# Attention scores on half the array's rows, and operand stacks copied inside SBUF

## The chip, the cores and the metric

One core of a Trainium2 chip runs the whole kernel. The metric is the device time of one launch in microseconds. TensorE, VectorE (DVE), ScalarE (ACT), GpSimd (POOL) and the DMA queue of SyncE (SP) each take their instructions in program order and wait for each other through semaphores.

## What is computed

The input x has 2048 tokens of 128 numbers. First comes causal attention with 16 heads of 8 dimensions, then a residual and a layer norm, then a mixture of 8 experts (each token goes to its best one) with a shared expert, a residual and a second layer norm. The change is in the attention:

```python
q, k, v = proj(Wq, bq), proj(Wk, bk), proj(Wv, bv)     # 16 heads of 8
scores = einsum('bhqd,bhkd->bhqk', q, k) / sqrt(8)     # masked: k_pos > q_pos
m = max(scores, axis=-1)
p = softmax(scores - m)
out = einsum('bhqk,bhkd->bhqd', p, v) @ Wo.T + bo
```

## The kernel before

Tokens go in 4 blocks (B) of 512, heads in 4 groups (g) of 4; a step is one group of one block (s = 4 B + g). q and k are float32, but the matmuls of scores take bf16: each number is split into three bf16 parts (ScalarE writes the first from the projection's PSUM bank, line 830; VectorE the other two, lines 942 to 947), and all nine products of parts are summed by stacking: q_stack and k_stack hold, per head, 9 x 8 = 72 rows (STACK), each row a part of one dimension. Three more rows hold the three bf16 parts of the row maxima, against rows of -1 in k_stack, so that one matmul gives scores minus maximum. 96 rows are contracted (KROWS); the rows from 64 on are filled beforehand (line 677, 680 on POOL, 932 on VectorE).

The stacks are built by DMA from SP's queue: send() writes the three parts of a side to memory (parts_dram, line 565), stack_q() reads them back in three DMAs of 24 rows (line 580), stack_k() in nine of 8 rows (line 591). Block 0 goes in two groups, heads 0 to 3 first. send(0, 1) and send(1, 1) follow; block 1's stack_q and stack_k are put on the queue after the maxima of step 0.

Each step runs through these items:

- scores (line 1230): for 128 queries t, a block c of up to 512 keys and a pair of heads hp, two matmuls q_stack x k_stack into two PSUM banks; on the diagonal (c == B) each is followed by a mask matmul of 128 columns (line 1233). VectorE takes the maxima of both banks (line 966). 320 such jobs, 288 of them in blocks 1 to 3.
- maxima: VectorE combines them (line 974), POOL splits them in three parts (lines 721, 726).
- maxrows: TensorE turns the parts (line 1241), ScalarE copies them to max_rows (line 850), SP sends them into q_stack (line 619).
- probs (line 1254): keys on the partitions, one matmul per head; ScalarE takes the exponential (line 843). It is scores minus maximum, recomputed in the other orientation. POOL masks the diagonal ones (line 710).
- values (line 1271): four heads at once, in four tiles of 32 columns of the array, f32.

make_plan writes one order for all of it: it goes through the probs items, each with a due count of score jobs (from columns, not from times), and lets a model of the engines' clocks choose between the next score job and the next main item. Every engine follows this order. SP follows it too, so a DMA waits on the queue for what stands before it:

```python
sp.wait_ge(max_rows_kept, s + 1)
sp.dma_start(q_stack[STACK:STACK + PARTS, B % 2, 4 * g:4 * g + 4, :], max_rows[:, s % 2, :])
if s == 0:
    stack_q(1, slice(0, H), q_stacked[1])
    stack_k(1, slice(0, H), k_stacked[1])
```

Of the kernel before, what the change touches and what calls it, by code (L numbers as in the profile page):

```python
# [28 lines left out]
JOB_COLUMNS = 60  # L29
LAST_RATE = 1.3  # L30
# [20 lines left out]
def make_plan(NB, G):  # L51
# [55 lines left out]
    plan, job, turns = [], 0, 0  # L107
# [17 lines left out]
    def put(item):  # L125
# [4 lines left out]
        if kind == "scores":  # L130
            _, m, B, g, t, c, hp = item
            w = width(B, t, c)
            clock["tensor"] += 0.84 * w + 8 + 107 * (c == B)
# [7 lines left out]
        elif kind == "probs":  # L141
            w = BLK - P * max(0, item[4] - TPB * item[2])
            clock["tensor"] += 0.42 * w + 3
# [4 lines left out]
        elif kind == "values":  # L148
            clock["tensor"] += 1.83 * (BLK - P * max(0, item[4] - TPB * item[2]))
        elif kind in costs:  # L150
            tensor, reader, read, after = costs[kind]
            clock["tensor"] += tensor
# [41 lines left out]
def block_kernel(nc, x, Wq, bq, Wk, bk, Wv, bv, Wo, bo, router_w, w_gate, w_up, w_down,  # L194
# [22 lines left out]
    SCALE = float(HD) ** -0.5  # L217
    STACK = PARTS * PARTS * HD
    KROWS = 96
    VC = HD + 1  # L220
    assert D == P and H * HD == D and STACK + PARTS <= KROWS
# [105 lines left out]
    with ctx:  # L327
# [24 lines left out]
        max_parts = sb("max_parts", [P, 2, TPB, PARTS, 4], BF16)  # L352
# [64 lines left out]
        parts_dram = nc.dram_tensor("parts_dram", (2, NB, PARTS, P, BLK), BF16, kind="Internal").ap()  # L417


# [22 lines left out]
        first_q_stacked = sem("first_q_stacked")  # L442
        first_k_stacked = sem("first_k_stacked")
# [17 lines left out]
        q_sent = [sem(f"q_sent{b}") for b in range(NB)]  # L461
        k_sent = [sem(f"k_sent{b}") for b in range(NB)]
# [77 lines left out]
        STACKED = 16  # L540
        CLEARED = 16
# [9 lines left out]
        def _(sp):  # L551
            sp.dma_start(x_sb[:, 0:TPB, :], x_tiles[:, 0:TPB, :]).then_inc(x_loaded[0], 16)
            sp.dma_start(w_nat[:, 1, :], Wk).then_inc(qk_loaded, 16)
            sp.dma_start(bias_qk[:, 1:2], bk.rearrange("(h d) -> d h", d=HD),
                         allow_slow_non_contiguous=True).then_inc(bias_qk_loaded, 16)
# [6 lines left out]
            def send(side, b):  # L562

                sp.wait_ge((q_split, k_split)[side], b + 1)
                sp.dma_start(parts_dram[side, b].rearrange("a p t -> p a t"),
                             qk_parts[:, side, b % 2, :, :]).then_inc((q_sent, k_sent)[side][b], 16)

            def stack_q(b, heads, stacked):

                sp.wait_ge(q_filled, min(b, 1) + 1)  # L570
                if b >= 2:

                    sp.wait_ge(exp_in_ready, units_before[b - 1])

                    sp.dma_start(q_stack[STACK:STACK + PARTS, b % 2, :, :],
                                 q_stack[STACK + PARTS:STACK + 2 * PARTS, b % 2, :, :]).then_inc(stacked, 16)
                sp.wait_ge(q_sent[b], 16)
                rows = parts_dram[0, b].rearrange("a (o d h) t -> o (a d) h t", o=1, d=HD)[:, :, heads, :]
                for r in range(PARTS):
                    sp.dma_start(q_stack[r * PARTS * HD:(r + 1) * PARTS * HD, b % 2, heads, :].rearrange("p h t -> p (h t)"),  # L580
                                 rows.rearrange("o p h t -> (o p) (h t)")).then_inc(stacked, 16)

            def stack_k(b, heads, stacked):

                sp.wait_ge(k_filled, b + 1)
                sp.wait_ge(k_sent[b], 16)
                for r in range(PARTS):
                    rows = parts_dram[1, b, r].rearrange("(d h) t -> d h t", d=HD)[:, heads, :].rearrange("d h t -> d (h t)")
                    for a in range(PARTS):
                        at = (r * PARTS + a) * HD  # L590
                        sp.dma_start(k_stack[at:at + HD, b, heads, :].rearrange("p h t -> p (h t)"), rows).then_inc(stacked, 16)
# [816 lines left out]
```

## Time and profile before

| | us |
|---|---|
| median of 3 runs | 608.11 (606.51 to 609.79) |
| profiled execution, its own time | 612.24 |
| its span, first to last instruction | 610.50 |
| TensorE / VectorE / ScalarE / POOL busy | 550.3 / 456.6 / 356.8 / 150.7 |

The rows further down come from the profiled execution. A busy time is the time in which an engine had at least one instruction under way; matmuls overlap, so the start times of neighbouring rows tell more of TensorE's pace than their lengths. PEclk is the granted clock of TensorE as a share of 2.4 GHz; the other level is 1.2 GHz, 0.50. "PEld" is the loading of weights, "SPq" the issue of a DMA on SP's queue. L1230 is line 1230 of the kernel before.

### The profile page before, as it was taken

What the parts mean: (1) busy time and instruction counts of PE and PEld (TensorE: products, weight loads), DVE (VectorE), ACT (ScalarE), POOL (GpSimd) and SP (SyncE); (2) the same over time, 40 slices, a digit from 0 to 9 for tenths busy, and PEclk for the clock granted to TensorE, in tenths of its full rate; (3) what the DMA queues carried; (4) which work ended last, traced back from release to release, by engine and by line L of the source; (5) the groups of instructions that cost most, each with busy time, mean ns of one, the idle gap of its engine ahead of it and who ended that gap; (6) DMA issues with size and microseconds to landing.
All of it is one profiled execution on the core that took longest, in us unless ns stands there. A gap on an engine that the chain in (4) does not pass through costs nothing.

```text
span 610.5 us, 10445 instructions
## 1 busy us (share of the span) xinstructions
PE 550.3 (90%) x3497; PEld 233.8 (38%) x3497; DVE 456.6 (75%) x765; ACT 356.8 (58%) x803; POOL 150.7 (25%) x267
## 2 busy tenths in 40 slices
PE   5539599999999999999999999999999899998980
PEld 3224234434333334333333333333434225664460
DVE  5728378999989988888888878888872515777684
ACT  3003355746567766877777776767778884331350
POOL 5651123130211202111001101101003157215644
PEclk9655789999999999999999999999999999999995
DMA  5736300036200045100000000000000111211233
GB/s 125 170 59 112 47 1 2 28 96 115 55 1 28 1 119 115 31 2 18 12 1 28 1 1 28 2 1 2 1 1 20 35 32 48 51 37 52 43 68 90
DMA packets 22909, 25.62 MB, mean 42 GB/s; under 512 B 2987, under 2 KB 21363, under 8 KB 22275
## 3 DMA queue, kind: packets, MB, share of 16 engines
q1 hardware_dynamic: 20896, 21.67, 15.2%
q0 software_dynamic: 1536, 3.15, 2.9%
q8 instruction: 29, 0.48, 0.3%
q14 instruction: 24, 0.19, 0.1%
q10 hardware_dynamic: 424, 0.13, 0.1%
HBM read 17.44 MB, written 7.21 MB: 40 GB/s over the span
## 4 chain that ended last, share of the span: by engine, by line
PE 73%; DVE 10%; DMA 6%; issue 5%; POOL 3%; ACT 2%; SPq 0%; POOLq 0%; DVEq 0%; ACTq 0%
PE out_ps L1271 21%; PE score_ps L1230 19%; PE ring_ps L1254 19%; DVE part_max L966 5%; DMA q_stack<-max_rows 3%; PE score_ps L1360 3%; PE score_ps L1233 2%; PE ring_ps L1377 1%; PE ring_ps L1280 1%; POOL k_stack L789 1%; PE score_ps L1312 1%; POOL qk_parts L776 1%; PE score_ps L1254 1%; PE ring_ps L1195 1%; PE ring_ps L1241 1%
## 5 line engine op out<-in xcount | busy, mean ns | idle before, releaser
L966 DVE TENSOR_REDUCE part_max<-score_ps 128x2 f32<-128x1024 f32 (+3 forms) x320 | 327.7, 1062 | 75.3 <-PE score_ps L1233 45.8
L843 ACT ACTIVATE probs<-ring_ps 128x512 f32<-128x512 f32 (+3 forms) x611 | 285.1, 537 | 123.9 <-PE ring_ps L1254 121.8
L1230 PE MATMUL score_ps<-k_stack,q_stack 96*128 96x512 bf16 (+3 forms) x640 | 182.3, 364 | 19.0 <-issue 10.5
L1254 PE MATMUL ring_ps<-q_stack,k_stack 96*128 96x512 bf16 (+3 forms) x611 | 172.9, 353 | 7.4 <-DMA q_stack<-max_rows 5.7
L1271 PE MATMUL out_ps<-probs,v_aug 128*32 128x512 f32 (+3 forms) x1280 | 150.7, 543 | 4.3 <-POOL probs L710 3.8
L1230 PEld LDWEIGHTS score_ps<-k_stack,q_stack 96*128 96x128 bf16 x640 | 60.5, 101 | 107.9 <-DVE part_max L966 39.2
L1254 PEld LDWEIGHTS ring_ps<-q_stack,k_stack 96*128 96x128 bf16 x611 | 52.1, 98 | 120.3 <-ACT probs L843 69.4
L710 POOL TENSOR_SCALAR_AFFINE_SELECT probs<-probs 128x512 f32<-128x512 f32 x64 | 40.6, 634 | 165.2 <-ACT probs L843 165.0
L1233 PE MATMUL score_ps<-mask_qk,ident_bf 128*128 128x128 bf16 x256 | 57.1, 241 | 0.0
L1271 PEld LDWEIGHTS out_ps<-probs,v_aug 128*32 128x32 f32 x1280 | 25.4, 108 | 49.6 <-issue 23.8
L721 POOL CAST max_parts<-row_max 128x16 bf16<-128x16 f32 x48 | 9.4, 196 | 117.7 <-DVE row_max L974 115.6
L776 POOL DMA_INDIRECT qk_parts<-xs_dram,q_stack x30 | 30.6, 1021 | 25.6 <-DVE q_stack L1093 17.7
L731 POOL TENSOR_TENSOR rstd<-rstd,minus_half 128x1 f32<-128x1 f32 x16 | 8.9, 554 | 103.3 <-DVE rstd L926 103.3
L1360 PE MATMUL score_ps<-w_gu,qk_parts 128*128 x60 | 32.0, 615 | 0.0
L850 ACT ACTIVATE max_rows<-ring_ps 12x512 bf16<-12x512 f32 x15 | 8.8, 584 | 39.0 <-PE ring_ps L1241 38.8
L1233 PEld LDWEIGHTS score_ps<-mask_qk,ident_bf 128*128 128x128 bf16 x256 | 27.6, 108 | 6.9 <-issue 0.9
L896 ACT ACTIVATE qk_parts<-score_ps 128x256 f32<-128x256 f32 x30 | 11.5, 384 | 29.3 <-PE score_ps L1360 29.3
L1111 DVE SCALAR_TENSOR_TENSOR qk_parts<-qk_parts,score_ps 128x256 f32<-128x256 f32 x30 | 12.6, 419 | 15.1 <-ACT qk_parts L896 15.0
L789 POOL DMA_INDIRECT k_stack<-sorted_dram,q_stack x16 | 16.9, 1054 | 15.3 <-DMA sorted_dram<-q_stack 10.6
L1377 PE MATMUL ring_ps<-wd,q_stack 128*128 x116 | 18.7, 284 | 0.2
L1377 PEld LDWEIGHTS ring_ps<-wd,q_stack 128*128 128x128 f32 x116 | 15.2, 191 | 1.6 <-issue 0.9
L877 ACT ACTIVATE k_stack<-score_ps 128x512 f32<-128x512 f32 x8 | 4.8, 597 | 18.0 <-PE score_ps L1312 18.0
(179 smaller groups left out, 417.6 us busy)
## 6 DMA issues: line engine op xcount, KB each, us to landing
q_stack<-parts_dram SPq DMA_DIRECT2D x9, 384.0 KB
k_stack<-parts_dram SPq DMA_DIRECT2D x27, 128.0 KB
parts_dram<-qk_parts SPq DMA_DIRECT2D x8, 384.0 KB, 2.7
sorted_dram<-q_stack SPq DMA_DIRECT2D x30, 64.0 KB, 1.5
x_sb<-in_L_attn_x_dram SPq DMA_DIRECT2D x4, 256.0 KB, 5.2
w_gu<-n_L_ffn_expert_gate_dram SPq DMA_DIRECT2D x8, 128.0 KB, 2.2
w_gu<-in_L_ffn_expert_up_dram SPq DMA_DIRECT2D x8, 128.0 KB, 2.4
wd<-n_L_ffn_expert_down_dram SPq DMA_DIRECT2D x8, 128.0 KB, 2.3
```

The costliest lines, as they stand in the source:

```text
L710: pool.affine_select(out=square, in_=square, compare_op=ALU.is_ge, fill=0.0, base=0, pattern=[[0, 4], [1, P]], channel_multiplier=-1).then ...
L776: pool.indirect_dma_start(out=xg[:, k % 8, :], out_offset=None, in_=xs_dram[0:P * tiles[w][1], :], in_offset=bass.IndirectOffsetOnAxis(ap= ...
L789: pool.indirect_dma_start(out=yg[:, t, :], out_offset=None, in_=sorted_dram[w][:, :], in_offset=bass.IndirectOffsetOnAxis(ap=slot_i[:, t:t ...
L843: act.activation(probs[:, n % RING, 0:w], bank(it)[:, 0:w], ACT.Exp, scale=SCALE).then_inc(probs_ready, 1)
L966: dve.tensor_reduce(out=part_max[:, s % 2, t, 2 * hp:2 * hp + 2, c], in_=score_ps[:, m % 2, :, 0:w], axis=AX.X, op=ALU.max).then_inc(score ...
L1111: link(dve.scalar_tensor_tensor(out=x_hid[:, k % 4, :], in0=x_hid[:, k % 4, :], scalar=1.0, in1=both[:, 0:FF], op0=ALU.add, op1=ALU.mult))
L1230: last = mm(score_ps[:, m % 2, i, 0:w], q_stack[0:KROWS, B % 2, h, t * P:(t + 1) * P], k_stack[0:KROWS, c, h, 0:w], start=True, stop=c < B)
L1233: last = mm(score_ps[:, m % 2, i, w - P:w], ident_bf[:, :], mask_qk[:, :], start=False, stop=True)
L1254: mm(bank(it)[:, 0:w], k_stack[0:KROWS, j // TPB, h, j % TPB * P:(j % TPB + 1) * P], q_stack[0:KROWS, B % 2, h, skip:BLK], start=True, sto ...
L1271: last = mm(out_ps[32 * i:32 * i + 32, skip:BLK], v_aug[:, j, h * VC:h * VC + 32], probs[:, (4 * k + i) % RING, 0:w], start=j == 0, stop=j ...
L1360: mm(bank(it), xgT[:, k % 4, :], w_gu[:, bass.ds(e, 1), :].rearrange("p a n -> p (a n)"), start=True, stop=True).then_inc(gate_up_made, 1)
L1377: last = mm(bank(it)[:, 0:D], x_hidT[:, k % 2, f * P:(f + 1) * P], wd[:, bass.ds(e, 1), f, :].rearrange("p a n -> p (a n)"), start=f == 0, ...
```

## The change

Two things change together, since both come from how the stacks lie.

The stacks are copied inside SBUF. send() and parts_dram are gone; stack_block(b) issues, for each of the three parts, each side, each half of the heads (x) and each of the three places where the part occurs, one DMA of 64 partitions x 512 bf16 into 8 rows x 8 heads x 512: 36 DMAs of 64 KB a block. It starts with the part that ScalarE writes, as soon as that stands, and ends with the smallest. Block 0 is no longer split into two groups of heads.

The heads lie in two halves. Heads 0 to 7 keep rows 0 to 95; heads 8 to 15 have their 72 rows at 56 to 127, with the maxima at 53 to 55 and the rest filled (zeros against -1). In each half the eight products of parts without the smallest one lie in 64 rows of one half of the array (0 to 63, 64 to 127). The score matmuls, which serve the maxima alone, contract only these 64 rows, and a job pairs a head of the lower half with one of the upper half. The mask matmuls come after both. Probs still contract all rows (96 or 128). max_rows goes into q_stack in two DMAs instead of one. The planner's clock charges 107 ns (DRAIN) where the tile shape changes, and 0.42 instead of 0.84 ns per score column.

```diff
-            clock["tensor"] += 0.84 * w + 8 + 107 * (c == B)
+            clock["tensor"] += drain(64, P if c == B else 64) + 0.42 * w + (DRAIN + 107) * (c == B)
...
-            clock["tensor"] += 1.83 * (BLK - P * max(0, item[4] - TPB * item[2]))
+            clock["tensor"] += drain(32, 32) + 1.67 * (BLK - P * max(0, item[4] - TPB * item[2]))
...
+    HALF = H // 2
+    LOW_TOP = 96
+    UP_AT = P - STACK
+    def head(g, i):
+        return 2 * g + i % 2 + HALF * (i // 2)
+    def rows_of(h):
+        return slice(0, LOW_TOP) if h < HALF else slice(0, P)
...
-            sp.dma_start(bias_qk[:, 1:2], bk.rearrange("(h d) -> d h", d=HD),
-                         allow_slow_non_contiguous=True).then_inc(bias_qk_loaded, 16)
+            for x in range(2):
+                sp.dma_start(bias_qk[64 * x:64 * (x + 1), 1:2], bk[64 * x:64 * (x + 1)].rearrange("(h d) -> d h", d=HD),
+                             allow_slow_non_contiguous=True).then_inc(bias_qk_loaded, 16)
...
+            def stack_block(b):
+                for part in reversed(range(PARTS)):
+                    for side in range(2):
+                        to, stacked = ((q_stack, q_stacked), (k_stack, k_stacked))[side]
+                        if part == PARTS - 1:
+                            sp.wait_ge(first_part_kept, 2 * b + side + 1)
+                        else:
+                            sp.wait_ge((q_split, k_split)[side], (PARTS - 1) * b + PARTS - 1 - part)
+                        if side == 0 and b >= 2:
+                            sp.wait_ge(exp_in_ready, units_before[b - 1])
+                        if part == 0:
+                            sp.wait_ge((q_filled, k_filled)[side], 2 * (min(b, 1), b)[side] + 2)
+                        for x in range(2):
+                            for other in reversed(range(PARTS)):
+                                r, a = ((other, part), (part, other))[side]
+                                at = (r * PARTS + a) * HD
+                                at = (at - HD) % STACK if x == 0 else UP_AT + at
+                                sp.dma_start(to[at:at + HD, (b % 2, b)[side], HALF * x:HALF * (x + 1), :],
+                                             qk_parts[64 * x:64 * (x + 1), side, b % 2, part, :]).then_inc(stacked[b], 16)
...
-            send(0, 0)
-            send(1, 0)
-            stack_q(0, slice(0, 4), first_q_stacked)
-            stack_k(0, slice(0, 4), first_k_stacked)
-            stack_q(0, slice(4, H), q_stacked[0])
-            stack_k(0, slice(4, H), k_stacked[0])
-            send(0, 1)
-            send(1, 1)
+            stack_block(0)
...
-                    sp.dma_start(q_stack[STACK:STACK + PARTS, B % 2, 4 * g:4 * g + 4, :],
-                                 max_rows[:, s % 2, :]).then_inc(max_rows_placed[s % 2], 16)
+                    sp.dma_start(q_stack[STACK:STACK + PARTS, B % 2, 2 * g:2 * g + 2, :],
+                                 max_rows[0:2 * PARTS, s % 2, :]).then_inc(max_rows_placed[s % 2], 16)
+                    sp.dma_start(q_stack[UP_AT - PARTS:UP_AT, B % 2, HALF + 2 * g:HALF + 2 * g + 2, :],
+                                 max_rows[2 * PARTS:4 * PARTS, s % 2, :]).then_inc(max_rows_placed[s % 2], 16)
                     if s == 0:
-                        stack_q(1, slice(0, H), q_stacked[1])
-                        stack_k(1, slice(0, H), k_stacked[1])
+                        stack_block(1)
...
-                    pool.memset(q_stack[64:96, 1, :, :].bitcast(F32), 0.0).then_inc(q_filled, 1)
+                    pool.memset(q_stack[64:96, 1, 0:HALF, :].bitcast(F32), 0.0).then_inc(q_filled, 1)
+                    pool.memset(q_stack[0:64, 1, HALF:H, :].bitcast(F32), 0.0).then_inc(q_filled, 1)
...
-                act.activation(wT[:, i, :].rearrange("p (d h) -> p d h", d=HD),
-                               score_ps[:, 1, 0, i * D:(i + 1) * D].rearrange("p (h d) -> p d h", d=HD), ACT.Copy).then_inc(w_kept, 1)
+                for x in range(2):
+                    half = slice(i * D + 64 * x, i * D + 64 * (x + 1))
+                    last = act.activation(wT[:, i, 64 * x:64 * (x + 1)].rearrange("p (d h) -> p d h", d=HD),
+                                          score_ps[:, 1, 0, half].rearrange("p (h d) -> p d h", d=HD), ACT.Copy)
+                last.then_inc(w_kept, 1)
...
-                    if B == 0 and g == 0 and t == 0:
-                        pe.wait_ge(first_k_stacked, STACKED * PARTS * PARTS)
-                        pe.wait_ge(first_q_stacked, STACKED * PARTS)
-                    elif g == (1 if B == 0 else 0) and t == 0:
-                        pe.wait_ge(k_stacked[c], STACKED * PARTS * PARTS)
-                        pe.wait_ge(q_stacked[B], STACKED * PARTS + (CLEARED if B >= 2 else 0))
-                    for i in range(2):
-                        h = 4 * g + 2 * hp + i
-                        last = mm(score_ps[:, m % 2, i, 0:w], q_stack[0:KROWS, B % 2, h, t * P:(t + 1) * P],
-                                  k_stack[0:KROWS, c, h, 0:w], start=True, stop=c < B)
-                        if c == B:
+                    if g == 0 and t == 0:
+                        pe.wait_ge(k_stacked[c], STACKED)
+                        pe.wait_ge(q_stacked[B], STACKED)
+                    for i, half in enumerate((slice(0, 64), slice(64, P))):
+                        h = head(g, 2 * i + hp)
+                        last = mm(score_ps[:, m % 2, i, 0:w], q_stack[half, B % 2, h, t * P:(t + 1) * P],
+                                  k_stack[half, c, h, 0:w], start=True, stop=c < B)
+                    if c == B:
+                        for i in range(2):
                             last = mm(score_ps[:, m % 2, i, w - P:w], ident_bf[:, :], mask_qk[:, :],
                                       start=False, stop=True)
```

## Rows read from the trace of the kernel before

**Rows 1.** Page, engines over the span: busy us, share, instructions

```profile
PE 550.3 (90%) x3497; PEld 233.8 (38%) x3497; DVE 456.6 (75%) x765; ACT 356.8 (58%) x803; POOL 150.7 (25%) x267
```

**Rows 2.** Busy time by stage: stretch, its length, engines; clock, DMA share, GB/s

```profile
20.00:80.00 60.00, 38.90 (x216) 18.70 (x217) 32.70 (x47) 11.77 (x27) 24.09 (x42) 0.59 0.46 85
130.00:182.00 52.00, 49.66 (x347) 21.06 (x345) 47.87 (x73) 31.32 (x72) 9.77 (x22) 1.00 0.35 71
283.00:455.00 172.00, 171.90 (x1115) 61.16 (x1114) 144.43 (x160) 127.14 (x264) 16.48 (x40) 1.00 0.03 8
73.40:80.00 6.60, 6.57 (x32) 2.81 (x33) 2.85 (x4) 3.87 (x8) 0.63 (x1) 0.50 0.01 2
```

**Rows 3.** Chain of waits, 20 to 80 us: start us, us, what

```profile
19.71 2.06 DMA k_stack<-parts_dram
...
30.32 9.14 issue
...
52.68 20.62 DMA q_stack<-max_rows
```

**Rows 4.** Timeline of TensorE in the steady stage: start us, us, what

```profile
308.60 0.64 PE L1271 MATMUL out_ps<-probs,v_aug 128*32 128x256 f32 x8
309.17 0.39 PE L1254 MATMUL ring_ps<-q_stack,k_stack 96*128 96x512 bf16 x1
...
312.90 0.38 PE L1254 MATMUL ring_ps<-q_stack,k_stack 96*128 96x512 bf16 x1
313.21 1.06 PE L1271 MATMUL out_ps<-probs,v_aug 128*32 128x512 f32 x8
314.21 0.61 PE L1230 MATMUL score_ps<-k_stack,q_stack 96*128 96x512 bf16 x2
314.65 0.38 PE L1254 MATMUL ring_ps<-q_stack,k_stack 96*128 96x512 bf16 x1
```

**Rows 5.** Groups by shape, line 1230: count, busy us, mean ns, idle before

```profile
L1230 PE MATMUL score_ps<-k_stack,q_stack 96*128 96x512 bf16 x448 | 135.9, 389 | 0.5 <-DVE part_max L966 0.2
...
L1230 PE MATMUL score_ps<-k_stack,q_stack 96*128 96x128 bf16 x64 | 12.2, 247 | 17.8 <-issue 10.5 <-DMA k_stack<-parts_dram 5.2 <-DVE part_max L966 2.0
```

**Rows 6.** SP's DMA queue, 10 to 135 us: start us, issue us, what

```profile
17.04 2.97 SPq L591 DMA_DIRECT2D k_stack<-parts_dram  x9
...
44.38 0.83 SPq L619 DMA_DIRECT2D q_stack<-max_rows  x1
...
46.59 3.07 SPq L591 DMA_DIRECT2D k_stack<-parts_dram  x9
...
131.75 0.71 SPq L575 DMA_DIRECT2D q_stack<-q_stack  x1
```

**Rows 7.** Stretches by what their DMA does; columns as in rows 2

```profile
17.25:20.75 3.50, 0.00 (x0) 0.00 (x0) 3.36 (x9) 0.00 (x0) 0.27 (x1) 0.96 0.34 95
46.00:48.00 2.00, 1.60 (x8) 0.59 (x6) 1.99 (x2) 0.00 (x0) 0.00 (x0) 0.50 0.81 189
60.00:68.00 8.00, 6.26 (x50) 2.37 (x48) 6.39 (x7) 3.55 (x11) 2.83 (x8) 1.00 0.51 71
415.55:415.75 0.20, 0.20 (x3) 0.08 (x2) 0.00 (x0) 0.20 (x1) 0.00 (x0) 1.00 0.18 61
```

**Rows 8.** Timelines of the first 80 us, four engines

```profile
8.71 0.69 ACT L830 ACTIVATE qk_parts<-ring_ps,bias_qk 128x512 bf16<-128x512 f32 x1 [2.23 <-PE ring_ps L1195]
...
13.71 0.43 DVE L947 CAST qk_parts<-qk_f 128x512 bf16<-128x512 f32 x1
...
30.34 0.18 DVE L974 TENSOR_REDUCE row_max<-part_max 128x16 f32<-128x16 f32 x1
...
38.81 0.20 POOL L721 CAST max_parts<-row_max 128x16 bf16<-128x16 f32 x1
...
67.11 0.64 PE L1271 MATMUL out_ps<-probs,v_aug 128*32 128x256 f32 x8 [1.23 <-POOL probs L710]
73.43 1.01 PE L1254 MATMUL ring_ps<-q_stack,k_stack 96*128 96x512 bf16 x2 [5.68 <-DMA q_stack<-max_rows]
```

More of the change, by code:

```diff
@@ L106, in make_plan, with drain @@
     slots, ring, exp_done, max_ready, max_placed = [0.0, 0.0], [0.0] * 3, {}, {}, {}
-    plan, job, turns = [], 0, 0
+    plan, job, turns, tiles = [], 0, 0, P
+    def drain(before, after):
+        nonlocal tiles
+        last, tiles = tiles, after
+        return DRAIN if before != last else 0
     def start_of(item):
@@ L142, in put @@
             w = BLK - P * max(0, item[4] - TPB * item[2])
-            clock["tensor"] += 0.42 * w + 3
+            clock["tensor"] += drain(P, P) + 0.42 * w + 3
             clock["scalar"] = max(clock["scalar"], clock["tensor"] + LATENCY) + 0.83 * w + 52
@@ L560, in _ @@
                              x_tiles[:, TPB * b:TPB * b + TPB, :]).then_inc(x_loaded[b], 16)
[L562 to L591, printed above, removed]
+            def stack_block(b):
[17 more added lines that the diff above has]
+                                             qk_parts[64 * x:64 * (x + 1), side, b % 2, part, :]).then_inc(stacked[b], 16)
@@ L717, in _ @@
                         pool.wait_ge(max_turned, s - 1)
-                    rest = row_max[:, s % 2, :, :]
+                    rest = row_max[:, s % 2, :, :].rearrange("p t (x j) -> p t x j", x=2)
                     for a in range(PARTS):
-                        part = max_parts[:, s % 2, :, a, :]
+                        part = max_parts[:, s % 2, :, :, a, :]
                         copied = pool.tensor_copy(part, rest)
@@ L826, in _ @@
                     if b == 0:
-                        act.wait_ge(bias_qk_loaded, 32)
+                        act.wait_ge(bias_qk_loaded, 64)
                     if b >= 2:
-                        act.wait_ge((q_sent, k_sent)[side][b - 2], 16)
-                    act.activation(qk_parts[:, side, b % 2, 0, :], bank(it), ACT.Identity,
+                        act.wait_ge((q_stacked, k_stacked)[side][b - 2], STACKED)
+                    act.activation(qk_parts[:, side, b % 2, PARTS - 1, :], bank(it), ACT.Identity,
                                    bias=bias_qk[:, side:side + 1]).then_inc(first_part_kept, 1)
@@ L941, in _ @@
                     parts = qk_parts[:, side, b % 2, :, :]
-                    dve.scalar_tensor_tensor(out=rest, in0=bank(it), scalar=bias_qk[:, side:side + 1], in1=parts[:, 0, :],
+                    dve.scalar_tensor_tensor(out=rest, in0=bank(it), scalar=bias_qk[:, side:side + 1], in1=parts[:, 2, :],
                                              op0=ALU.add, op1=ALU.subtract).then_inc(qk_kept, 1)
                     dve.wait_ge(qk_kept, 2 * b + side + 1)
-                    link(dve.tensor_copy(parts[:, 1, :], rest))
+                    split = (q_split, k_split)[side]
+                    dve.tensor_copy(parts[:, 1, :], rest).then_inc(split, 1)
+                    dve.wait_ge(split, (PARTS - 1) * b + 1)
                     link(dve.tensor_tensor(rest, rest, parts[:, 1, :], ALU.subtract))
-                    dve.tensor_copy(parts[:, 2, :], rest).then_inc((q_split, k_split)[side], 1)
+                    dve.tensor_copy(parts[:, 0, :], rest).then_inc(split, 1)
                 elif kind == "v_in":
@@ L1249, in _ @@
                     w = BLK - skip
-                    h = 4 * g + i
+                    h = head(g, i)
                     wait_bank(it)
                     if j == 0 and i == 0:
-                        pe.wait_ge(max_rows_placed[s % 2], 16 * (s // 2 + 1))
-                    mm(bank(it)[:, 0:w], k_stack[0:KROWS, j // TPB, h, j % TPB * P:(j % TPB + 1) * P],
-                       q_stack[0:KROWS, B % 2, h, skip:BLK], start=True, stop=True).then_inc(exp_in_ready, 1)
+                        pe.wait_ge(max_rows_placed[s % 2], 32 * (s // 2 + 1))
+                    mm(bank(it)[:, 0:w], k_stack[rows_of(h), j // TPB, h, j % TPB * P:(j % TPB + 1) * P],
+                       q_stack[rows_of(h), B % 2, h, skip:BLK], start=True, stop=True).then_inc(exp_in_ready, 1)
                 elif kind == "values":
```

54 lines of the change are left out of this document (24 added, 30 removed).

## The prediction, made before the change was run

> **What bounds the kernel now.** I read the page's engine table first [rows 1]: TensorE is busy for 90% of the span, VectorE for 75%, ScalarE for 58%. That is an average over stages, so next came the busy time by stage [rows 2]. From 283 to 455 us TensorE is busy for 171.90 of 172 us at the full clock, with VectorE at 84% and ScalarE at 74%: there only TensorE's own work counts, and a microsecond taken from it is a microsecond of the span as long as less than 16% goes. From 130 to 182 us it is busy for 96% and VectorE for 92%. From 20 to 80 us the picture is another one: TensorE 65%, a granted clock of 0.59, DMA busy. The chain of waits says why [rows 3]. The first scores wait for the DMA of the k stack until 21.8; then 9.14 us are waited for the other heads' stack (shown as "issue"); and from 52.68 to 73.30 one small DMA, the maxima of step 1 on their way into q_stack, takes 20.62 us, because block 1's stack was put on the same queue before it. So the change has two places to act in, and they are priced apart: the start (DMA) and the scores of blocks 1 to 3 (TensorE).
>
> **The scores.** TensorE streams the 512-column score matmuls 0.215 us apart (314.21 to 314.65 for two) [rows 4]. There are 448 such matmuls and 64 each of 384, 256 and 128 columns (the first and the last of four groups in [rows 5]), 278,528 columns; 20,480 are block 0's (32 jobs, two heads, four widths), so blocks 1 to 3 have 258,048, or 504 times 512. Two heads at once takes away half of that: 252 x 0.215 = 54.2 us, if the two halves truly run side by side. The trace has a pattern for that: the values put four heads in four column tiles of the array, and four 128x512 f32 matmuls of 0.6 us each, in two passes, end within 1.06 us [rows 4].
>
> The same rows price the other side. A 512-column probs matmul is followed by the next one after 0.215 us, but by values after 0.31 (312.90 to 313.21): 0.095 us to enter the other tile shape. The next matmul starts 1.00 us after values of 512 columns and 0.57 us after values of 256 (308.60 to 309.17); the line through the two has 1.68 ns a column and 0.14 us at zero columns, which is the price of leaving. So a switch costs 0.095 to 0.14 us; I take 0.11, nearer to the entry, since the exit also holds the staggered start of four tiles. The page TensorEngine Tiling (Array Packing) of the Trainium skill says under Key Properties that a change of the tiling mode, and not merely of the tile, drains TensorE; the trace agrees with these 0.095 us. Without that rule the scores part would be the whole 54 us.
>
> How many switches are new? The order that make_plan writes for the kernel before has 254 separate runs of score jobs in blocks 1 to 3 for 288 jobs: nearly every job stands alone between probs. Only 62 of the run ends touch values, where the array switches anyway. In blocks 1 to 3 the order has 313 changes of tile shape now; with scores in half-height tiles, and the mask matmuls of the 96 diagonal jobs in the full shape, the same order has 784. That is 471 new ones: 51.8 us at 0.11 (44.7 at 0.095, 65.9 at 0.14). The planner's due times count columns, which the diff leaves alone, so I expect about the same order. Against 54.2 us saved this is a gain of 2 us, between a gain of 10 and a loss of 12. If the second half had to wait for its own weight load, up to 0.055 us a job would come on top (16 us for 288); mask matmuls of 128 columns follow each other at such a pace with a weight load each, and that load can hide under the first half, so I take nothing and keep it as a bound.
>
> **The stack copies.** Per block the send, three q and nine k DMAs (with the split of block 0 into two groups) become 36 copies of 64 KB, 2304 KB as before. Three prices set how long they take.
> Issue: nine k copies took 2.97 and 3.07 us on SP's queue, 0.33 each; but the two kinds of DMA inside SBUF that the trace has, max_rows and the clearing of q_stack, took 0.83 and 0.71 [rows 6]. These go from three rows, so the cause may be the odd count. Bounds: 12 and 27 us for 36.
> Transfer: the k copies go to 8 rows at a time and use 8 of 16 DMA engines, as the new ones will; while only they ran they moved 71 GB/s (60 to 68 us, share 0.51) [rows 7]: 33 us for a block. The small first group went at 95 GB/s with share 0.34, held by issue. The one SBUF-to-SBUF row, max_rows in 1 KB pieces as in the new copies, moved 61 GB/s at a share of 0.18, 21 GB/s an engine: 8 engines would need 14 us.
> So a block takes 14 to 33 us. I take 20, between the nearest in kind (max_rows) and the nearest in pattern (k).
>
> With 20 us, step by step: q's first part stands at 9.40 and the last part of k at 14.14 [rows 8]; the second wT and bias pieces add some 0.5 us, so the copies run from 9.9 to 30 and land at 32 (2 us as in [rows 3]). That is later than the 21.8 of before, but all heads are there, and the 9.14 us wait is gone: step 0's scores took 8.5 us (21.8 to 30.34), so step 1 starts near 40, as it does now (30.32 + 9.14). POOL's fills and maxima, done at 39.0 [rows 8], cover nothing any more; POOL does the same fills in two halves each, at the same cost. max_rows of step 0 goes out near 45, now as two DMAs (0.8 us more); then SP issues block 1's copies, 46.4 to 66.4, and the maxima of step 1, queued behind them on SP and in the rings, land at 68.4 instead of 73.3. TensorE, whose last work before the stall ends at 67.8 [rows 8], then hardly waits: 5 us gained, and 2 more because the clock need not fall: after 5.68 us of standing still [rows 8] it was granted 0.50, that is 1.2 of 2.4 GHz, from 73.4 to 80, with TensorE busy all the time [rows 2]. For blocks 2 and 3 the copies have some 25 us before the next maxima are used, and the scores there wait for VectorE; nothing. Later max_rows DMAs cost 0.8 us of SP each, under those leads; if the lead were gone it would be 14 x 0.8 = 11 us. VectorE's and GpSimd's instructions keep their sizes.
>
> **Sum.** 2 us from the scores and 7 from the start: 9 us. The profiled execution has its own time of 612.24 us (span 610.50, 1.74 around it); 612.24 - 9 = 603.2. It lies 4.1 us above the median of the three runs, 608.11, so the median becomes 599.
>
> **The rivals.**
> A, the copies keep pace with issue: 14 us a block. First scores at 26, step 1's maxima in place at 58 and no stall; TensorE reaches that point at 63, as POOL at 39.0 holds step 0's maxima. That is 10 us, 3 for the clock and 2 from the scores: 593, down to 585 with switches at 0.095. The max_rows row speaks for it, the k rows against it.
> B, the slower end: the copies crowd into 8 rows each, in at 71 GB/s, or SP needs 0.75 us for each; 31 us a block. First scores at 43, block 1's copies from 57 to 88, step 1's maxima at 90: 16 us later than now, so 608 + 16 - 2 = 622. It decides from about 24 us a block on, where the landing (28 us and two blocks' copies after the start) passes 76. For it speaks that q's copies, to 24 rows, moved 189 GB/s (share 0.81) where k's, to 8, moved 71 [rows 7]; against it the 95 GB/s of the first group. The page SBUF — State Buffer of the Trainium skill (Door 1: The DMA port swizzle) has bandwidth follow the number of SBUF ports that a range of partitions reaches; by its 27 GB/s a port the two ports of 8 rows would give an estimated 43 us a block. The k rows, at 71 GB/s, lie above that and below q's.
> C, the two halves do not overlap, so the scores' part of the change does not do what it says: 52 us of switches for nothing, less 7: 653. The values' overlap speaks against it.
> D, a switch costs 0.14 us or the second weight load shows: a loss of 12 to 16 in blocks 1 to 3, less 7 at the start: 615.
>
> **How the numbers follow.** Forecast 0.40 (592 to 605), A 0.22, B 0.20, D 0.13, C 0.05. The range of 585 to 622 leaves out C, the half of B with still slower copies (0.10), and 0.04 at the foot of A. A change under 0.5% (3 us) is about what a measurement here cannot tell from none. Faster: A, and nearly all of the forecast: 0.60; same: the forecast's upper edge and the near edges of B and D: 0.10; slower: the rest, 0.30.
>
> **What would show it.** First scores at 32 us (A 26, B 43), and a 36-copy block of 20 us on SP; the DMA wait for max_rows near nothing in the chain, and a clock that stays up through 80 us. In the steady stage two score matmuls of one job starting together, gaps of about 0.1 us before and after each job, and TensorE still busy throughout, so a stretch that shrinks by little. Wrong it would be with SBUF copies far from 20 us a block, or gaps away from 0.11 us: 0.01 us of a gap is 5 us of the kernel.

## The result and the profile of the changed kernel

| | kernel before | changed kernel |
|---|---|---|
| median of 4 runs, us | 607.62 | 635.08 |
| ratio, with its 95% interval | | 1.0455 (1.0408 to 1.0502) |
| profiled execution, us | 612.24 | 632.4 |
| its span, us | 610.50 | 630.7 |

The change makes the kernel slower by 27.5 us where 9 us of gain were forecast. The two profiled executions lie nearer together than the medians (before's 4.6 us above its median, this one 2.7 below): the two traces hold 20.2 us of the loss. The kernel before spreads from run to run, most on the chip of the experiments with rows 8 apart (598.4 to 613.0 us), and a ratio with its interval may leave out longer runs, so that it can differ from the quotient of the medians.

Busy time by stage of the changed kernel, the stretches that [rows 2] show of before (columns: stretch, length, busy us of TensorE, its weight loads, VectorE, ScalarE and GpSimd; granted clock, DMA share, GB/s):

```profile
20.00:80.00 60.00, 29.59 (x168) 9.96 (x168) 27.15 (x41) 7.21 (x15) 22.16 (x41) 0.54 0.41 51
130.00:182.00 52.00, 42.92 (x277) 14.44 (x276) 40.76 (x58) 25.17 (x54) 7.40 (x18) 0.90 0.49 68
283.00:455.00 172.00, 171.10 (x1146) 48.98 (x1148) 146.89 (x165) 127.54 (x269) 19.02 (x44) 1.00 0.03 8
```

The steady stage is as full as it was. The two stages in which copies run are not: TensorE has 9.3 us less work done by 80 us and 6.7 us less between 130 and 182, where it was busy for 49.66 of 52 us before. SP's queue says when the copies go (start, time to issue, what):

```profile
9.40 3.98 SPq L593 DMA_DIRECT2D q_stack<-qk_parts  x6
...
29.18 3.89 SPq L593 DMA_DIRECT2D k_stack<-qk_parts  x6
58.27 0.79 SPq L611 DMA_DIRECT2D q_stack<-max_rows  x1
59.10 0.73 SPq L613 DMA_DIRECT2D q_stack<-max_rows  x1
59.88 3.98 SPq L593 DMA_DIRECT2D q_stack<-qk_parts  x6
...
84.31 0.76 SPq L611 DMA_DIRECT2D q_stack<-max_rows  x1
...
139.42 4.00 SPq L593 DMA_DIRECT2D q_stack<-qk_parts  x6
...
159.47 3.90 SPq L593 DMA_DIRECT2D k_stack<-qk_parts  x6
163.41 0.77 SPq L611 DMA_DIRECT2D q_stack<-max_rows  x1
...
178.03 0.72 SPq L611 DMA_DIRECT2D q_stack<-max_rows  x1
...
435.54 0.72 SPq L611 DMA_DIRECT2D q_stack<-max_rows  x1
```

The 36 copies of a block take 23.7 us to issue, 0.65 us each, and they land later than that by the chain of waits (start, us, what):

```profile
32.46 13.73 DMA k_stack<-qk_parts
...
85.11 5.60 DMA q_stack<-max_rows
...
158.75 13.03 DMA q_stack<-qk_parts
```

Block 0's last copy lands at 46.2, 13.7 us after it was issued and 36.8 us after the first: 2304 KB (2.36 MB) at 64 GB/s. A backlog has built up behind the issue. The first scores start at 46.3, the maxima of step 1 land at 90.7 (before: 73.3 [rows 3]), and block 2's copies land at 171.8 with TensorE waiting. In TensorE's timeline (start, us, what, then in brackets its idle time before and what ended that):

```profile
46.29 0.29 PE L1229 MATMUL score_ps<-k_stack,q_stack 64*128 64x128 bf16 x2 [29.76 <-DMA k_stack<-qk_parts]
...
171.91 0.61 PE L1229 MATMUL score_ps<-k_stack,q_stack 64*128 64x512 bf16 x2 [6.91 <-DMA q_stack<-qk_parts]
```

The maxima's DMAs, one step after the other, are milestones for where the loss arises. SP's queue of the kernel before (steps 5, 7 and 14), then step 5 of the changed kernel, whose others stand above:

```profile
114.34 0.70 SPq L619 DMA_DIRECT2D q_stack<-max_rows  x1
...
155.16 0.72 SPq L619 DMA_DIRECT2D q_stack<-max_rows  x1
...
414.20 0.72 SPq L619 DMA_DIRECT2D q_stack<-max_rows  x1
```

```profile
128.55 0.69 SPq L611 DMA_DIRECT2D q_stack<-max_rows  x1
```

Step 0's went out at 44.38 before [rows 6] and at 58.27 now: 13.9 us later. Step 5's is 14.2 us later, step 7's 22.9, step 14's 21.3, the end 20.2. So 14 us are lost at the start, some 9 more between steps 5 and 7, where block 2's stack is late, and then 2.7 us come back.

### The profile page after: what moved, and what is told of

Read it like the earlier page. It is cut to its first block, busy times and chain, and to the rows that moved or that the text cites. A ratio compares the mean times of both kernels' runs of the same rounds, so it can differ in the third digit from the quotient of the medians.

```text
span 630.7 us, 10545 instructions
## 1 busy us (share of the span) xinstructions
PE 545.3 (86%) x3497; PEld 198.0 (31%) x3497; DVE 455.7 (72%) x766; ACT 357.7 (57%) x805; POOL 151.0 (24%) x272
## 4 chain that ended last, share of the span: by engine, by line
PE 64%; SPq 10%; DVE 9%; DMA 7%; issue 4%; POOL 3%; ACT 2%; POOLq 0%; DVEq 0%; ACTq 0%
PE out_ps L1271 19%; PE ring_ps L1254 18%; PE score_ps L1229 11%; SPq L593 9%; DVE part_max L967 5%; PE score_ps L1233 3%; PE score_ps L1361 2%; DMA k_stack<-qk_parts 2%; DMA q_stack<-qk_parts 2%; PE ring_ps L1378 1%; PE ring_ps L1281 1%; POOL k_stack L783 1%; DMA q_stack<-max_rows 1%; PE score_ps L1313 1%; PE ring_ps L1196 1%
## 5 line engine op out<-in xcount | busy, mean ns | idle before, releaser
L1254 PE MATMUL ring_ps<-q_stack,k_stack 128*128 128x512 bf16 (+7 forms) x611 | 177.0, 358 | 2.1 <-ACT probs L841 1.3
L1229 PE MATMUL score_ps<-k_stack,q_stack 64*128 64x512 bf16 (+3 forms) x640 | 115.5, 371 | 50.3 <-DMA k_stack<-qk_parts 29.8
L1254 PEld LDWEIGHTS ring_ps<-q_stack,k_stack 96*128 96x128 bf16 (+1 forms) x611 | 48.6, 98 | 126.6 <-ACT probs L841 78.4
L1229 PEld LDWEIGHTS score_ps<-k_stack,q_stack 64*128 64x128 bf16 x640 | 29.7, 94 | 152.5 <-issue 86.7
L1233 PE MATMUL score_ps<-mask_qk,ident_bf 128*128 128x128 bf16 x256 | 40.0, 243 | 0.0
L770 POOL DMA_INDIRECT qk_parts<-xs_dram,q_stack x30 | 30.6, 1019 | 25.6 <-DVE q_stack L1094 17.7
L1233 PEld LDWEIGHTS score_ps<-mask_qk,ident_bf 128*128 128x128 bf16 x256 | 15.1, 100 | 23.6 <-issue 18.5
L841 ACT ACTIVATE probs<-score_ps 128x512 f32<-128x512 f32 (+3 forms) x29 | 15.2, 553 | 0.1
```

Source lines behind the costliest of these rows:

```text
L770: pool.indirect_dma_start(out=xg[:, k % 8, :], out_offset=None, in_=xs_dram[0:P * tiles[w][1], :], in_offset=bass.IndirectOffsetOnAxis(ap= ...
L841: act.activation(probs[:, n % RING, 0:w], bank(it)[:, 0:w], ACT.Exp, scale=SCALE).then_inc(probs_ready, 1)
L1229: last = mm(score_ps[:, m % 2, i, 0:w], q_stack[half, B % 2, h, t * P:(t + 1) * P], k_stack[half, c, h, 0:w], start=True, stop=c < B)
L1233: last = mm(score_ps[:, m % 2, i, w - P:w], ident_bf[:, :], mask_qk[:, :], start=False, stop=True)
L1254: mm(bank(it)[:, 0:w], k_stack[rows_of(h), j // TPB, h, j % TPB * P:(j % TPB + 1) * P], q_stack[rows_of(h), B % 2, h, skip:BLK], start=Tru ...
```

## The experiments

**The two halves of the change, one at a time.** The first kernel keeps the scores from 64 rows and builds the stacks through memory (`stack` reads a side's parts back into the new rows, for the given heads of each half):

```
+            def send(side, b):
+                sp.wait_ge((q_split, k_split)[side], (PARTS - 1) * (b + 1))
+                for x in range(2):
+                    sp.dma_start(parts_dram[side, b, x].rearrange("a p t -> p a t"),
+                                 qk_parts[64 * x:64 * (x + 1), side, b % 2, :, :]).then_inc((q_sent, k_sent)[side][b], 16)
...
-            stack_block(0)
+            send(0, 0)
+            send(1, 0)
+            stack(0, 0, 0, 2, first_q_stacked)
+            stack(1, 0, 0, 2, first_k_stacked)
+            stack(0, 0, 2, HALF, q_stacked[0])
+            stack(1, 0, 2, HALF, k_stacked[0])
...
```

> The scores from 64 rows, two heads at once, are kept; the stack rows go through memory again as in the kernel before (three q and nine k reads for each half of the heads, 25 reads a block where before had 12, with 8 KB a row in place of 16). Theory 1, the copies are the whole loss and the scores are worth next to nothing: 598 to 612 us, first scores near 32 us, TensorE again at 48 to 50 busy us of 52 in the second block's stage, and the steady stage 2 us shorter than before's. Rival, the half-height scores cost as well (a switch dearer than the 0.105 us that the timeline of the changed kernel shows): 615 to 630 us, and the distance from step 6 to step 15 longer than before's.

Measured: 606.99 us against 609.2 of before beside it, ratio 0.9967 (0.9931 to 1.0002). The scores, with the reads that their layout asks for, cost nothing; a gain of 2 us is not clear of none. So nothing in the loss is theirs. The second kernel keeps the copies and scores full rows:

```
-                    for i, half in enumerate((slice(0, 64), slice(64, P))):
+                    for i in range(2):
                         h = head(g, 2 * i + hp)
-                        last = mm(score_ps[:, m % 2, i, 0:w], q_stack[half, B % 2, h, t * P:(t + 1) * P],
-                                  k_stack[half, c, h, 0:w], start=True, stop=c < B)
+                        last = mm(score_ps[:, m % 2, i, 0:w], q_stack[rows_of(h), B % 2, h, t * P:(t + 1) * P],
+                                  k_stack[rows_of(h), c, h, 0:w], start=True, stop=c < B)
```

> The part-by-part copies are kept; the scores contract the full rows of each head (96 or 128) as before, one head after the other, so there is no change of tile shape. For blocks 2 and 3 the rows still hold the maxima of two blocks ago, so the output isn't the reference's. Theory 1, the loss is all the copies': 632 to 642 us, first scores near 46 us, TensorE waiting again for block 2's stack near 160 to 172 us. Rival, the loss is in the scores: 605 to 615 us.

Measured: 635.57 us (one of the four runs took 627.47), ratio 1.0385 (1.0310 to 1.0459). The loss is the copies'.

**What makes a copy slow: issue, source or destination.** One kernel changes only where a copy writes:

```
-                                sp.dma_start(to[at:at + HD, (b % 2, b)[side], HALF * x:HALF * (x + 1), :],
+                                n = PARTS * (PARTS - 1 - part) + PARTS - 1 - other
+                                h, low = (HALF * x + n, x == 0) if n < HALF else (HALF * (1 - x), x == 0)
+                                sp.dma_start(to[0 if low else 64:64 if low else P, (b % 2, b)[side], h, :],
                                              qk_parts[64 * x:64 * (x + 1), side, b % 2, part, :]).then_inc(stacked[b], 16)
```

> The same 36 copies a block of 64 KB from the same rows, but each is written to 64 rows of 1 KB (one head's columns) in place of 8 rows of 8 KB; the stacks then hold the wrong data, so the output isn't the reference's. Theory 1, eight destination rows are what limits the rate: a block's copies land 2 to 3 us after the last issue, first scores at 35 to 38 us in place of 46, DMA above 90 GB/s while they run, 612 to 624 us. Rival 2, a copy inside SBUF in 1 KB pieces is slow wherever it lands: first scores again at 45 to 47 us and 630 to 637 us.

Another only where it reads (the sends to memory ahead of it are left out here):

```
...
                                 sp.dma_start(to[at:at + HD, (b % 2, b)[side], HALF * x:HALF * (x + 1), :],
-                                             qk_parts[64 * x:64 * (x + 1), side, b % 2, part, :]).then_inc(stacked[b], 16)
+                                             parts_dram[side, b, x, part].rearrange("(d h) t -> d h t", d=HD)).then_inc(stacked[b], 16)
```

> The parts are sent to memory part by part (12 sends of 64 KB a block) and read back by the same 36 DMAs a block, into the same eight rows each; only the source differs from the changed kernel. Theory 1, the eight destination rows are the limit: a block's 36 reads take 30 to 37 us as the copies did (2304 KB at 62 to 75 GB/s), first scores at 46 to 52 us, 630 to 642 us. Rival 2, SBUF as the source in 1 KB pieces is the limit: the reads take 14 to 25 us, first scores at 34 to 42 us, 610 to 625 us.

Measured: 608.71 us with 64 destination rows, 638.24 us from memory (one run each). The first scores of the kernel with 64 rows, in TensorE's timeline (start, us, what, idle before it and what ended that):

```profile
33.88 0.29 PE L1231 MATMUL score_ps<-k_stack,q_stack 64*128 64x128 bf16 x2 [17.26 <-DMA k_stack<-qk_parts]
```

and of the kernel that reads from memory, its reads in SP's queue and its first scores:

```profile
17.35 2.17 SPq L602 DMA_DIRECT2D q_stack<-parts_dram  x6
...
27.81 1.95 SPq L602 DMA_DIRECT2D k_stack<-parts_dram  x6
```

```profile
47.96 0.29 PE L1238 MATMUL score_ps<-k_stack,q_stack 64*128 64x128 bf16 x2 [28.15 <-DMA k_stack<-parts_dram]
```

With the same source and the same issue, 64 rows let the block land 2 us after the last issue. With the same eight rows but half the issue time (0.33 us each, all issued by 29.8), reading from memory still takes 30.5 us to land, 77 GB/s. So the destination is the limit; SBUF as a source and SP's 0.65 us make at most some 6 of the 37 us. One rival is left: the copies to 64 rows also run on more DMA engines. From 15 to 30 us their trace has 14 or more packets (single pieces of a DMA) under way at once for a third of the time; the changed kernel never has 14, and mostly 8 to 10. The next kernel settles it: it keeps eight rows a copy, has mostly 4 to 9 packets under way and never 14.

**Eight rows, or eight rows side by side.** The order of a stack's rows is free as long as q and k share it. So row 8 n + d can become row 8 d + n:

```
-                                sp.dma_start(to[at:at + HD, (b % 2, b)[side], HALF * x:HALF * (x + 1), :],
+                                if x == 0:
+                                    rows = slice(at // HD, STACK - HD, HD) if at < STACK - HD else slice(at, at + HD)
+                                else:
+                                    rows = slice(64 + (at - 64) // HD, P, HD) if at >= 64 else slice(at, at + HD)
+                                sp.dma_start(to[rows, (b % 2, b)[side], HALF * x:HALF * (x + 1), :],
                                              qk_parts[64 * x:64 * (x + 1), side, b % 2, part, :]).then_inc(stacked[b], 16)
```

> The changed kernel, with the rows of the stack in another order, the same for q and k: each copy still writes 8 rows of 8 KB from the same 64 rows, but its rows stand 8 apart (row 8 d + n in place of 8 n + d), for 8 of the 9 copies of a half. Theory 1a, it is 8 rows side by side that share a way into SBUF: first scores at 34 to 38 us, block 2 without a stall, 604 to 614 us, as with 64 rows. Rival 1b, it is the number of rows (or the 8 KB that each gets) wherever they stand: first scores at 45 to 47 us again, 629 to 637 us.

Measured: 609.43 us, against 608.67 of before beside it, ratio 1.0033 (0.9996 to 1.0070); its trace spans 607.9 us, before's 610.5, the changed kernel's 630.7. The order of the rows takes back the loss, as far as the spread of before's runs on that chip lets one say (609.43 lies 6 us above the median of its eight shortest). Busy time from 15 to 30 us, while block 0's copies run, first of the changed kernel, then with rows 8 apart (the last three columns: clock, DMA share, GB/s):

```profile
15.00:30.00 15.00, 1.53 (x10) 1.05 (x8) 5.29 (x12) 1.20 (x2) 9.35 (x6) 0.68 0.58 68
```

```profile
15.00:30.00 15.00, 4.90 (x12) 2.68 (x12) 5.33 (x13) 1.51 (x3) 6.91 (x4) 0.76 0.37 103
```

The copies move 103 GB/s in place of 68, and now at the pace of the issue (64 KB in 0.64 us is 102 GB/s), while the DMA engines are busy less, 0.37 against 0.58. A packet of 1 KB took 143 ns in the median of that stretch in the changed kernel, 46 ns with rows apart. First scores at 35.3, block 2 without a stall:

```profile
35.30 0.29 PE L1233 MATMUL score_ps<-k_stack,q_stack 64*128 64x128 bf16 x2 [15.12 <-DMA k_stack<-qk_parts]
```

```profile
130.00:182.00 52.00, 49.54 (x350) 17.70 (x352) 49.10 (x75) 32.02 (x74) 10.03 (x23) 1.00 0.19 54
```

How far apart must rows be? With a step of 2 (`slice(first, first + 2 * HD - 1, 2)`), 8 rows lie within 16:

> As the kernel with rows 8 apart, but with the 8 rows of a copy 2 apart, so that they lie within 16 rows. If what counts is how many groups of four neighbouring rows a copy touches (8 side by side touch two, 2 apart and 8 apart both four): first scores at 34 to 37 us as with 8 apart, 604 to 614 us. If the rows must lie far apart: first scores at 39 to 44 us, 615 to 630 us.

Measured: 610.49 us (one run), first scores at 35.7, and

```profile
15.00:30.00 15.00, 1.50 (x10) 1.05 (x8) 5.29 (x12) 1.16 (x2) 9.38 (x6) 0.67 0.36 100
```

Two apart does as well as eight apart. Both rates are held by the issue, so what the rows themselves would allow was not reached. (Eight rows 8 apart touch eight groups of four neighbouring rows, not four as the expectation counts; the two groups of eight rows side by side are the slow case either way.)

**The rest of the wait.** With rows apart the kernel stands about where it stood before the change. Three kernels let ScalarE send the maxima's rows, so that they don't stand behind block 1's copies on SP:

```
                     act.activation(max_rows[:, s % 2, :], bank(it)[0:4 * PARTS, :], ACT.Copy).then_inc(max_rows_kept, 1)
+                    B, g = divmod(s, G)
+                    act.wait_ge(max_rows_kept, s + 1)
+                    act.dma_start(q_stack[STACK:STACK + PARTS, B % 2, 2 * g:2 * g + 2, :],
+                                  max_rows[0:2 * PARTS, s % 2, :]).then_inc(max_rows_placed[s % 2], 16)
+                    act.dma_start(q_stack[UP_AT - PARTS:UP_AT, B % 2, HALF + 2 * g:HALF + 2 * g + 2, :],
+                                  max_rows[2 * PARTS:4 * PARTS, s % 2, :]).then_inc(max_rows_placed[s % 2], 16)
...
```

> The kernel with rows 8 apart, and the maxima's rows sent by ScalarE, right after it has written them, in place of SP: they no longer stand behind block 1's and block 2's copies in SP's queue. If spread rows are fast and the queue is what holds step 1's maxima: they land near 55 in place of 73 us, 596 to 604 us. If the shared DMA engines hold them: within 2 us of the kernel with rows 8 apart alone.

> The scores from 64 rows with the stacks through memory, and the maxima's rows sent by ScalarE. If the queue holds step 1's maxima: 594 to 602 us, 3 to 8 us below the same kernel with SP sending them. If the shared DMA engines do: within 2 us of it (604 to 609 us).

> The kernel before, with the maxima's rows sent by ScalarE in place of SP; nothing else. The 20.6 us from issue to landing of step 1's maxima were, by theory, a wait in SP's DMA queue behind block 1's 12 reads: landing within 6 us, 598 to 604 us. Rival, the DMA engines are shared by both queues and the wait stays: 605 to 610 us.

Measured: 626.26 us with rows apart (17 us worse than with SP sending), 622.47 with stacks through memory, and 609.71 for the kernel before (608.67 beside it); the ratios to the kernel before are 1.0280 (1.0197 to 1.0363), 1.0231 (1.0146 to 1.0316) and 1.0147 (1.0104 to 1.0191). Step 1's maxima did go out at 54.6 us in place of 72.8, as theory had it, but ScalarE paid for it at every step. Its queue in the kernel with rows apart, steps 11 and 13:

```profile
296.14 0.72 ACTq L852 DMA_DIRECT2D q_stack<-max_rows  x1
296.90 0.71 ACTq L854 DMA_DIRECT2D q_stack<-max_rows  x1
...
381.61 0.74 ACTq L852 DMA_DIRECT2D q_stack<-max_rows  x1
```

These two steps lie 85.47 us apart, against 82.92 with SP sending (284.61 to 367.53): 1.28 us a step for two DMAs of 0.72 us, or an estimated 19 us over 15 steps. The two issues keep ScalarE from the exponentials for 1.6 us, and TensorE waits for them, as here after step 11's:

```profile
298.37 0.39 PE L1261 MATMUL ring_ps<-q_stack,k_stack 128*128 128x512 bf16 x1 [1.80 <-ACT probs L842]
```

In the 4 us after each step's copy of the maxima TensorE stands still for 1.2 us in the mean of steps 6 to 14, and for 0.3 us in the kernel before with one send, which keeps ScalarE for 0.85 to 0.92 us: by these figures TensorE's lead covers one send, not two. So that kernel's steady stage keeps its pace (82.57 us for these two steps against 82.52). Its wait is gone as well: step 3's maxima go out 5.3 us earlier than before. In SP's queue before, and in ScalarE's now:

```profile
76.04 0.70 SPq L619 DMA_DIRECT2D q_stack<-max_rows  x1
```

```profile
70.71 0.72 ACTq L852 DMA_DIRECT2D q_stack<-max_rows  x1
```

Yet its time is no shorter. The first two kernels missed both of their ranges; the third lies in its rival's (605 to 610 us), but not for the rival's reason, since TensorE waits for no DMA there in its trace. Why these 5 us don't show in its median stays open.

Then block 0's issue was shared:

> Rows 8 apart, and block 0's 18 k copies issued by ScalarE while SP issues the 18 q copies; later blocks as before from SP. If, with the rows apart, SP's 0.64 us an issue is what is left (36 of them are 23 us): all of block 0 is issued by 26 us, first scores at 27 to 31 us in place of 35, 601 to 606 us. Rival, ScalarE's 18 issues hold up its own evictions (the weights that the values need, block 1's parts) by as much: 606 to 612 us.

> As the kernel with two queues, and block 1's copies go in thirds: 12 after the maxima's rows of step 0, 12 after those of step 1, 12 after those of step 2. If the rows of step 1's maxima cost what they stand behind SP's 36 issues: they are issued near 50 to 58 us in place of 73, and 3 to 6 us come off the kernel with two queues, 596 to 603 us. Rival, block 1's stack lands later and its scores wait for it instead: 604 to 610 us.

Measured: 618.75 us (1.0208, 1.0124 to 1.0291) and 620.86 us (1.0247, 1.0162 to 1.0331), both slower than either branch allowed, though the first scores came at 33.5 and 33.2. ScalarE's queue, and what GpSimd did after it:

```profile
10.72 13.23 ACTq L848 DMA_DIRECT2D k_stack<-qk_parts  x18
```

```profile
35.78 1.80 POOL L676 MEMSET q_stack<- 32x2048 f32 x1 [25.98 <-DVE qk_parts L967]
```

While ScalarE issues until 24 us, block 1's parts wait for its eviction; GpSimd waits for those parts before it fills block 1's rows, and its fills of three blocks then hold step 0's maxima until 53.6. It is the rival's mechanism, one engine longer than the rival had it. In thirds, the scores waited 7.4 us for block 1's stack as well.

The last kernel draws on these traces: ScalarE issues four groups of six (by block, side, part) only after its last early eviction, block 1 follows block 0 at once on both queues, and the fills of blocks 2 and 3 come after the maxima of steps 0 and 1.

```
+        by_scalar = ((0, 1, 1), (0, 1, 0), (1, 1, 1), (1, 1, 0))
...
             stack_block(0)
+            stack_block(1)
             for it in plan:
...
-                    if s == 0:
-                        stack_block(1)
...
+                    if it == ("k_in", 1):
+                        for group in by_scalar:
+                            copy_part(act, *group)
...
+                    if s < 2:
+                        pool.wait_ge(max_ready, s + 1)
+                        fill_k(s + 2)
```

> Rows 8 apart as before, and three moves at the start: ScalarE issues 24 of the 72 copies of blocks 0 and 1, and only after its last early eviction (20 us in the kernel with rows 8 apart; it then stands idle until 46); SP issues the other 48 one after the other, block 1's straight behind block 0's in place of behind step 0's maxima; GpSimd fills blocks 2 and 3 after the maxima of steps 0 and 1 in place of ahead of them. If SP's issue and the order in its queue are what is left of the copies' cost: first scores at 28 to 30 us in place of 35, step 0's maxima rows issued by 42 and step 1's by 50 us (47 and 74 with rows 8 apart), block 1's stack complete by 44, 590 to 600 us. Rival, the copies of two queues hold each other or the maxima's rows up, or ScalarE's issues run into step 0's maxima: 603 to 612 us.

Measured: 602.13 us against 608.03, ratio 0.9905 (0.9868 to 0.9941): 1% faster than the kernel before, 2 us short of the expected range and 1 us below the rival's. SP's queue:

```profile
44.68 0.79 SPq L624 DMA_DIRECT2D q_stack<-max_rows  x1
45.52 0.73 SPq L626 DMA_DIRECT2D q_stack<-max_rows  x1
52.17 0.69 SPq L624 DMA_DIRECT2D q_stack<-max_rows  x1
```

Step 1's maxima go out at 52.2 (72.8 with rows apart alone), and the 20.62 us wait of [rows 3] is gone from the chain. The first scores came at 32.7, not at 28 to 30: block 0's last copy took 5.45 us to land, with block 1's beside it, which is the rival's mechanism. Which of the three moves gives how much was not parted.

## Why the prediction was wrong, step by step

**The scores: right.** A gain of 2 us was forecast. The time of the scores alone (0.9967 of 609.2, from 4 us of gain to none) can't tell 2 from 0, but the traces bear it out: from step 7's maxima to the end the changed kernel takes 452.7 us, the kernel with the scores alone 453.9, the kernel before 455.3. TensorE's timeline of the changed kernel in the steady stage shows each term:

```profile
302.11 0.39 PE L1229 MATMUL score_ps<-k_stack,q_stack 64*128 64x512 bf16 x2
302.44 0.28 PE L1233 MATMUL score_ps<-mask_qk,ident_bf 128*128 128x128 bf16 x2
...
316.27 0.39 PE L1254 MATMUL ring_ps<-q_stack,k_stack 96*128 96x512 bf16 x1
316.60 0.39 PE L1229 MATMUL score_ps<-k_stack,q_stack 64*128 64x512 bf16 x2
316.92 0.61 PE L1254 MATMUL ring_ps<-q_stack,k_stack 96*128 96x512 bf16 x2
```

Two score matmuls take 0.39 us, as long as one: the halves overlap fully, and the second weight load does not show. From probs to scores are 0.33 us, from scores to the next 0.32 to 0.33, against 0.215 without a change of shape [rows 4]: 0.105 to 0.115 us a switch, where 0.11 was taken; and the changed kernel's order has 790 changes of shape in blocks 1 to 3, where 784 were counted. C (no overlap) and D (a dearer switch) fall.

**The copies: the step that failed.** "So a block takes 14 to 33 us. I take 20, between the nearest in kind (max_rows) and the nearest in pattern (k)." It takes 36.8 us, beyond the upper bound. The lower end came from dividing the rate of max_rows by its share of busy engines, 21 GB/s an engine, as if eight engines could each do that into eight rows. The rows refute it: with the destination rows moved apart the share fell from 0.58 to 0.37 while the rate rose from 68 to 103 GB/s. A share that falls while the rate rises counts waiting too (143 and 46 ns for a packet of the same size), so it is no measure of room left. The k rows' 71 GB/s [rows 7] were the row to go by; pattern beat kind. From memory into the same rows a block took 30.5 us, so the pieces of 1 KB from SBUF, or the slower issue at their start, may hold the other 6; no run parts these two. Issue, at 0.65 us, lay within its bounds and would have been 24 us alone.

The rule that the prediction weighed there, the Trainium skill's page SBUF — State Buffer (Door 1: The DMA port swizzle), gave an estimated 43 us for the two ports of 8 rows; 36.8 us lie between that and the k rows. By the same section of the Trainium skill four neighbouring rows share a port, and rows 32 apart do too, so that 8 rows 2 apart and 8 rows 8 apart both reach four ports. The trace agrees in that both moved more than the 68 GB/s of rows side by side, 100 and 103; that it is four ports, and that rows 32 apart share one, no run here shows, since issue held both rates.

**"For blocks 2 and 3 the copies have some 25 us [...]; nothing."** Right about the cover (TensorE runs out of other work at 165.0, 25.6 us after block 2's first issue), wrong for block 2 with the real size: its copies take 32.4 us (139.4 to 171.8), and the loss of some 9 us there is of the kind that the sum had at zero. Block 3's copies were hidden: they were issued by 264.8, the next maxima by 275.9, and TensorE was busy for 100.28 of the 101 us from 182 to 283.

**The maxima of step 1.** They were to land at 68.4, 5 us earlier; they land at 90.7. The order of events on SP's queue was right, only the block time was wrong that drove it twice. What TensorE stands still for there, though, is block 1's stack first, which its order has ahead of step 1's probs:

```profile
87.87 0.61 PE L1229 MATMUL score_ps<-k_stack,q_stack 64*128 64x512 bf16 x2 [8.98 <-DMA q_stack<-qk_parts]
```

After that the maxima cost it 0.16 us more. The 2 us for the clock fell with it: it was granted at 0.54 of full speed from 20 to 80 us, 0.59 before.

**The rivals.** B had the mechanism and its milestones: first scores at 43 (46.3), step 1's maxima at 90 (90.7). Its 622 us was too low because it left out block 2. Its turning point, "from about 24 us a block on", fits: with rows apart a block takes 25.8 us from its first issue (9.5) to its first scores (35.3), and the time is near that of the kernel before. It had 0.20 of the chance, and the forecast and A, which both rest on the max_rows row, 0.62. The range ended at B's 622 because the k rows were taken for its worst end; 13 us of the loss lie outside.

## What to carry to other kernels

Here a DMA's rate followed the rows that it wrote: take it from a row of the trace with the same destination pattern, and don't scale it by the share of busy engines, which was higher where the destination was crowded. Where the order of partitions is free, give each DMA rows that lie apart; here that was worth some 26 us by the medians (635.08 to 609.43, not measured side by side). And when a transfer's time is uncertain, price each place where it is used with the same doubt: a cover of 25 us is nothing to rely on when the transfer may take 37.

## What the runs showed of the hardware beyond that

- A copy of 64 KB inside SBUF in 1 KB pieces took 0.65 us to issue from SP and 0.73 from ScalarE; the same 64 KB from memory into rows of 8 KB took 0.33.
- Eight rows side by side took 64 GB/s from SBUF and 77 GB/s from memory, with many copies in flight; eight rows 2 or 8 apart, and 64 rows, took 100 to 104 GB/s, held by one queue's issue; with two queues issuing, eight rows 8 apart took 129 GB/s from 15 to 30 us.
- Two DMAs of 0.72 us issued by ScalarE at each step cost 1.28 us of the steady stage a step; one of 0.72 us a step cost nothing that shows in that stage.
